# Row forms for a second quad in two phases, and earlier emptying in the last two, in a routed-convolution kernel

## The reference, cut to what matters

```
x = x + L0(group_norm(x));  x = x + L1(group_norm(x))     # x: 32 images of 32 x 32 pixels, 64 channels

L0, 3 steps, per image:
    attn = softmax(q . k(x) / 4) over the 1024 pixels, 2 heads;  pooled = attn . v(x)
    weights = softmax(masked(pooled @ Wmlp) / 1.5);  keep the two largest of 4, rescale: wsel
    x_mod = x * (1 + mean_heads(attn) * 1024 * softplus(alpha))
    x = sum over experts e of wsel[e] * (conv3x3(x_mod, We[e]) + be[e])
    the first choice is barred in the next step (the last expert never is)
L1, involution: xi = x @ Wi + bi;  r = relu(batch_norm(x @ Wr + br));  w = r @ Ws + bs  (9 weights for each of 16 groups)
    out = sum over the 9 taps of w[tap] * shifted(xi)
```

## Time and profile before

| | |
|---|---|
| median of 3 runs | 675.14 us (674.09 to 675.57) |
| profiled execution, its own time | 673.33 us |
| its span, first to last instruction | 671.5 us |
| busy: TensorE, VectorE, ScalarE, GpSimd | 628.5, 522.5, 326.7, 181.0 us |
| mean granted TensorE clock | 0.985 |

### The profile page before, as it was taken

The page is one execution under the profiler, slowest core; times in us unless marked ns, Lnnn a source line. Parts: engine busy times, 40 slices in busy tenths (PEclk is TensorE's granted clock), DMA queues, the critical chain, the costliest instruction groups (busy, mean ns, idle before and its releaser), DMA issues. The chain is left out here.

```text
span 671.5 us, 15413 instructions
## 1 busy us (share of the span) xinstructions
PE 628.5 (94%) x5984; PEld 250.0 (37%) x5984; DVE 522.5 (78%) x816; ACT 326.7 (49%) x451; POOL 181.0 (27%) x193
## 2 busy tenths in 40 slices
PE   6868999889999999999999989798999999999995
PEld 7523333323333333333333323233444444444442
DVE  5699875997766666766688676969898898888885
ACT  3754632311422242133315545743687787788761
POOL 2100330007300810280047000531344234235231
PEclk9979899999999999999999979999999999999998
DMA  8930030042433253125422416000122222132132
GB/s 323 220 66 1 1 84 1 1 95 71 98 93 73 72 139 101 50 71 141 95 67 55 116 31 149 1 9 9 25 57 48 48 64 48 41 70 49 40 72 63
DMA packets 67461, 47.95 MB, mean 71 GB/s; under 512 B 53602, under 2 KB 54596, under 8 KB 67396
## 3 DMA queue, kind: packets, MB, share of 16 engines
q1 hardware_dynamic: 67108, 46.82, 28.3%
q10 hardware_dynamic: 288, 0.21, 0.1%
HBM read 35.15 MB, written 9.76 MB: 67 GB/s over the span
## 5 line engine op out<-in xcount | busy, mean ns | idle before, releaser
L759 PE MATMUL conv<-xpad,comb 64*64 64x512 f32 x2016 | 228.1, 597 | 4.3 <-DVE x L1386 4.2
L1646 DVE TENSOR_TENSOR x<-conv,x 128x512 f32<-128x512 f32 x288 | 177.9, 683 | 24.0 <-PE conv L814 22.7
L759 PEld LDWEIGHTS conv<-xpad,comb 64*64 64x64 f32 x2016 | 75.4, 134 | 136.6 <-issue 121.7
L814 PE MATMUL conv<-rstack,wse 98*128 98x512 f32 x288 | 95.9, 434 | 2.9 <-DVE xin L1432 0.9
L830 PE MATMUL att<-x,cmp 64*32 64x512 f32 x1280 | 79.7, 596 | 0.0
L814 PEld LDWEIGHTS conv<-rstack,wse 98*128 98x128 f32 x288 | 48.1, 188 | 72.3 <-DVE x L1646 65.7
L1318 DVE SCALAR_TENSOR_TENSOR xpad<-att,x 128x1024 f32<-128x1024 f32 x46 | 54.1, 1219 | 25.7 <-PE att L609 25.3
L960 ACT ACTIVATE x<-conv,bias 128x512 f32<-128x512 f32 x40 | 25.2, 682 | 90.5 <-PE conv L759 90.5
L728 PE MATMUL conv<-row_sums,comb 64*64 64x512 f32 x480 | 58.5, 617 | 9.0 <-DVE xin L1432 7.7
L1798 POOL TENSOR_TENSOR x<-x,xin 128x1024 f32<-128x1024 f32 x15 | 35.9, 2393 | 111.5 <-ACT x L1112 111.5
L951 ACT ACTIVATE comb<-experts,small 128x768 f32<-128x768 f32 (+1 forms) x33 | 27.4, 859 | 78.1 <-PE conv L728 31.9
(11 more groups left out here) (212 smaller groups left out, 749.8 us busy)
## 6 DMA issues: line engine op xcount, KB each, us to landing
experts<-forms SPq DMA_DIRECT2D x72, 192.0 KB, 4.0
experts<-forms SPq DMA_DIRECT2D x72, 144.0 KB, 2.8
x<-in_x SPq DMA_DIRECT2D x32, 256.0 KB, 5.6
out<-comb SPq DMA_DIRECT2D x30, 256.0 KB, 3.2
rstack<-rstack SPq DMA_DIRECT2D x16, 128.0 KB, 2.3
experts<-in_We SPq DMA_DIRECT2D x1, 1152.0 KB
forms<-experts SPq DMA_DIRECT2D x2, 576.0 KB, 5.7
out<-comb SPq DMA_DIRECT2D x4, 128.0 KB, 2.2
```

Of the source, the lines that this page charges most:

```text
L759: last = nc.tensor.matmul(conv[own[to], h, HW * rows:HW * rows + HW], comb[own[rows], q % 2, n, tap(t)], xpad[own[rows], 2 * (q % 2) + n, ...
L814: nc.tensor.matmul(conv[:, unit, cols], wse[:, ORDER[i], :], rstk[s][0:RR, cols], start=True, stop=True).then_inc(exp_full, 1)
L1646: v.tensor_tensor(img(prod[i])[:, rows, :], img(conv[:, unit, :])[:, rows, :], xip[s][:, kh + 16 * h:kh + 16 * h + 16, kw:kw + W], ALU.mul ...
```

## The change

`SHORT` takes in the second quad of phases 2 and 3 (quads 9 and 13), so that three short quads stand in a row there (8, 9, 10 and 12, 13, 14). With it come: the finish of the quad before is interleaved with the sum and the difference of the next (`sum_rows` now calls `finish_rows(q - 1, 0)` between them); the map of quad 9 moves from the third stage of quad 8 into the second, since `modulate(9)` now comes ahead of `middle_rows(8)`; the logits of the next phase move into the first stage of quad 9. In the last two phases `final(q, 0)` of quads 17, 19 and 21 is written ahead of the next quad's sums (for quad 19 ahead of the next modulate too), and `add_residual(q - 1)` right behind the finish of quad q - 1. On SyncE the gather of quad 22 is written ahead of the wait for a residual addition and of the transfers of the involution's constants.

```diff
-SHORT = tuple(QP * p + j for p in range(1, PHASES) for j in (0, 2))
+SHORT = tuple(QP * p + j for p in range(1, PHASES) for j in range(QP - 1) if j != 1 or p in (2, 3))
...
-            for q in range(GATHER_FROM, QP * LAST + 6):
+            for q in range(GATHER_FROM, QUADS - 1):
                 gather(q)
             eng.wait_ge(residual_added, residuals(QP * LAST + 2))
             for dst, src in LATE_CONSTS:
                 eng.dma_start(dst, src).then_inc(late_consts_in, 16)
-            for q in range(QP * LAST + 6, QUADS):
-                gather(q)
+            gather(QUADS - 1)
...
-                elif at == ((2, 0) if j == 0 else (1, 1)):
+                elif j == 1 and at == (0, 1):
+                    logits(p + 1)
+                elif at == ((2, 0) if j == 0 and q + 1 not in SHORT else (1, 1)):
                     attention_map(q + 1)
...
                     .then_inc(sums_ready, 1)
+                if q - 1 in SHORT:
+                    finish_rows(q - 1, 0)
...
                     if q - 1 in SHORT:
-                        finish_rows(q - 1, 1)
+                        if q not in SHORT:
+                            finish_rows(q - 1, 1)
...
+                    if q - 1 in SHORT_FINAL:
+                        add_residual(q - 1)
...
+                        if q - 1 in SHORT and q in SHORT and q + 1 in SHORT:
+                            middle_rows(q)
                         (combine_two if q + 1 >= GATHER_FROM else combine)(q + 1)
...
-                        if q in SHORT:
+                        if j == 0 and q + 1 in SHORT:
+                            modulate(q + 1)
+                        if q in SHORT and not (q - 1 in SHORT and q + 1 in SHORT):
                             middle_rows(q)
...
-                        modulate(q + 1)
-                        if q in SHORT:
+                        if q >= QP * LAST and q not in SHORT and j == 3:
+                            final(q, 0)
+                        if not (j == 0 and q + 1 in SHORT):
+                            modulate(q + 1)
+                        if q in SHORT and q + 1 not in SHORT:
                             finish_rows(q, 0)
+                        elif q >= QP * LAST and j < 3:
+                            final(q, 0)
                         if q + 1 in SHORT:
                             sum_rows(q + 1)
+                            if q in SHORT:
+                                finish_rows(q, 1)
                             subtract_rows(q + 1)
-                    if q >= QP * LAST and q not in SHORT:
+                    if q == QUADS - 1:
                         final(q, 0)
-                    if q - 1 in SHORT_FINAL:
-                        add_residual(q - 1)
-                    if q == QUADS - 1:
                         final_stats(q - 1)
```

## The result

The changed kernel takes 669.57 us, the median of 4 runs (668.44 to 670.36), beside 675.12 for the kernel before (674.09 to 675.57, 4 runs). The ratio is 0.9919, 95% interval 0.9900 to 0.9937. It is faster by 5.5 us; 670.4 was forecast, within 665.2 to 674.2. The profiled execution took 669.44 us, its span 667.7.

The account below looks back on a forecast made before the run. TensorE was taken as the bound overall, with VectorE's order deciding inside the phases. Late gain -9.3 plus 4.6 for the third and fourth phase gave -4.7 us: 668.6 on the profile's scale, 670.4 on the median's, range 665.2 to 674.2.

Parts of the forecast that it names:

- The late part: Last two phases: VectorE's reordering and the earlier gather remove TensorE's waits at quads 20 and 22, gain 9.3 us.
- Quad 20: Last phase: the 3.94 us wait and 2.6 us lost behind it go, a new 1.2 us wait comes; gain 5.5.
- Quads 21 and 22: Last phase: both waits of 1.88 us at quad 22 go, gain 3.8 us.
- The gather: SyncE: gather 22 moves ahead of the residual wait, so ScalarE's weights and modulate(22) come early; needed for quad 22's 3.8 us.
- Third and fourth phase: Row forms of quads 9 and 13: each phase 2.3 us longer (1.6 + 0.7), 4.6 in both.
- The chain: Third and fourth phase: VectorE needs some 13.8 us per row-form quad, TensorE 11.2; each phase 1.6 us longer.
- The clock term: Behind the 4.0 us wait quad 10 loses 1.7 to 2.6 us, 1.4 spare; 0.7 taken per phase.
- (2): Phases even: VectorE's chain 2 us shorter and the clock stays up, only -9.3, 665.8 us; chance 0.14.
- (1): TensorE-bound phases: VectorE's order does not matter, -20.1, 655.0 us; chance 0.04.
- (3): Dearer phases: whole clock loss comes through and GpSimd holds VectorE, 4.2 us each, -0.9, 674.2 us; chance 0.14.
- rival (4): Late gain half: moved residual or gather still late, quad 22 keeps its waits, -0.9, 674.2 us; chance 0.08.
- (5): Slower: clock at half through all of quad 10, 10.2 us a phase, +11, 686 us; chance 0.05.

Follow-up runs that it names:

- combine first: The changed kernel with VectorE's combining of quad 10's (14's) weights ahead of the middle rows of quad 9 (13): 667.39 us, ratio 0.9888.
- late part alone: The changed kernel with `SHORT` as before (no row forms for quads 9 and 13), all of the late part kept: 664.74 us, ratio 0.9871.

## Why the prediction was right, and where it was not

**The late part.** Forecast 9.3 us; 8.9 measured by itself, 10.0 in the changed kernel's trace up to quad 23. Quad 20: from the end of quad 19 to the start of quad 21 it was 403.57 - 385.54 = 18.0 us, and is 403.23 - 390.52 = 12.7, so 5.3, for which I had 5.5. The wait of 1.2 us for `final(19, 1)` came as 1.16, and the experiment that moves this call took it away. The clock was 1.00 from 385 to 398, as I had written. Quads 21 and 22: 31.9 us became 27.7, so 4.2 for my 3.8. The last 0.4 us lie in the fifth phase. The 0.8 us lost behind quad 23 I had counted at nothing.

**The gather: the step that was wrong.** I wrote that "the change lets gather 22 go ahead of that wait" and that this frees ScalarE. With the gather in its old place ScalarE isn't late: the residual addition that SyncE waited for 11.1 us has itself moved ahead, and that alone frees the gather. What the order on SyncE does decide is when ScalarE gets quad 22's weights, by 0.45 us, and through ScalarE when GpSimd starts. I had not looked at GpSimd in the last phase. That the late gain came out whole was luck in this point: in the changed kernel GpSimd starts at 414.42, 0.21 us behind VectorE's difference (414.21, 1.28 us long), and a start half a microsecond earlier cost 3.8 us in the late part.

**Third and fourth phase.** Forecast 4.6 us longer; 4.8 by itself, 5.2 in the trace. The chain was read rightly in its places: quad 8's last stage waits 1.40 us (1.4), and quad 10 waits 4.08 (4.0). Its size was too large, 1.03 us per phase for my 1.6: at full clock, with TensorE kept busy, quad 11 starts at 243.54, which is 243.4 on the old trace's clock, where I had 243.9. Quad 10 starts 0.3 us later than I had it, and from there to quad 11 it is 12.3 us in place of 13.2. Some 0.4 of that 0.9 is what I added for GpSimd's part: in the changed kernel quad 10's difference took 1.28 us (I had 1.46) and its subtractions 2.49 (2.7). The wait of 1.4 us that I expected inside quad 10 is 0.47 us at full clock; in the changed kernel it isn't there, since quad 10 ran slowly and VectorE waited for it instead (0.72 us).

The clock term was too small: 0.7 per phase for 0.81 and 2.33. I had 1.7 to 2.6 us lost behind the wait and 1.4 to spare. Measured, 40 records lost 1.34 us in the third phase (5.86 for 4.52) and 2.86 in the fourth (7.38), and 0.5 us of either was absorbed. So in the third phase the sum is right by luck, with the loss and the spare both too large; in the fourth, where the clock came back 5.8 us behind quad 14's start and not 2.8 us as behind quad 10's, the loss was above my range and most of it came through. The two errors nearly cancel, 1.1 us too much for the chain and 1.7 too little for the clock: that the 4.6 us of the forecast lie so near the 4.8 and 5.2 is luck as well.

**The rivals.** That the phases come out even (2) needs the clock and a shorter chain: with combine ahead of the middle rows it came true, 63.37 us at full clock. That TensorE bounds the phases (1) is refuted: less work on VectorE shortened the wait one for one, and no version of the triple went under 62.9 us. The dearer phases (3) wanted 4.2 us each; the fourth lost 3.4, by the chain and the clock and without a hold on VectorE. The wait in quad 22 of rival (4) appeared in two experiments, but by GpSimd's hold and not by a late residual or gather. The slower case (5), half clock through all of quad 10, did not occur.

**GpSimd beside VectorE, and the clock.** Holding between GpSimd and VectorE is larger than the rows of before showed (0.25 us). The Trainium skill (SBUF — State Buffer, section Who interferes with whom) has the loser blocked for a whole instruction; the 3.71 us for a difference (GpSimd's operation ended at 411.44, the difference 1.15 us later) and the 2.48 us for an operation on 32 columns agree with it. In the third and fourth phase, where I weighed that rule, VectorE's rows of the changed kernel show nothing of it, though GpSimd's routing ran beside them; there GpSimd's rows are the longer ones, 1.15 us for the cast (L1767, at 231.07) that took 0.20 before. For the clock (TensorE: Matmul & The Clock Gate, section What's actually happening), that activity releases the throttle: the kernel with repeated matmuls agrees.

**What stays open.** Why the clock fell for 3 us behind one wait of 4.08 us and for 7 us behind the other, and why it fell behind one wait of 2.52 us and not behind the other: no run separates that. Nor did I find what the 0.90 us wait for ScalarE behind quad 23 depends on, or why the sum of the two parts (4.1 us) is below the 5.5 us of the whole.

## What to carry to other kernels

Before work is shifted from the busiest engine to one with idle time on average, write out the other engine's order between two points at which the first waits: here 5.4 us less matmul work per phase became 1.8 to 3.4 us more time, because the receiving engine needed 13.8 us for a quad (VectorE from 221.79 to 235.62) where the giving one needed 11.2 (two stages in 5.59 us). A wait on TensorE costs more than its length once the clock falls behind it; filling it with matmuls that change nothing was a gain. And an edit that shifts GpSimd against VectorE by half a microsecond or less can bring or take 2.6 to 3.8 us: hold large GpSimd operations until a place where VectorE is not on the path.

## What was not expected of the hardware

- A GpSimd operation of 1152 elements stretched VectorE's difference from 1.28 to 3.71 us where it started 0.49 us ahead of it, and to 3.72 us where it started 0.05 us ahead (410.17 and 410.22, combine first); where it started 0.03 us ahead (409.24 and 409.27, late part alone) the difference took 1.28 us and the hold fell on the subtractions behind it, 4.80 for 2.5, which cost nothing.
- A GpSimd subtraction of 1088 elements took 2.5 us, VectorE's 1.24 (two in 5.04 and 2.48), and it held even a VectorE operation on 32 columns until its end.
- The granted clock behind like waits: it fell behind all four waits of 4.08 us (40 records took 5.86, 7.38, 6.22 and 6.18 us, at full clock 4.52) and both of 4.12 (24 records 5.39 and 4.51 us, at full clock 2.85), behind one of two waits of 2.52 us, two of four of 2.22 (6.22 us each), and neither of 1.46.
